# A separate tile for Gelu's quarters, and row spectra loaded for two pairs at a time, in a Fourier-operator kernel

## The reference, cut to what matters

```python
h = einsum('bhwi,ic->bhwc', x, fc0_w) + fc0_b            # 3 channels -> 64
for l in range(4):
    xf  = rfft2(h)
    top = einsum('bixy,ioxy->boxy', xf[:, :, :16, :16],  w1[l])   # mixes channels, mode by mode
    bot = einsum('bixy,ioxy->boxy', xf[:, :, -16:, :16], w2[l])
    sc  = irfft2(top and bot in a spectrum of zeros)
    y   = sc + einsum('bihw,oi->bohw', h, pw_w[l]) + pw_b[l]
    y   = (y - mean) * rsqrt(var + 1e-5) * gamma[l] + beta[l]     # mean, var of a channel over all images
    h   = gelu(y)
h   = gelu(h @ fc1_w + fc1_b)
out = h @ fc2_w + fc2_b
```

## Time and profile before

| | |
|---|---|
| median of 3 runs | 4079.1 us |
| the profiled execution | 4098.0 us |
| its span, first to last instruction | 4096.2 us |
| PE busy | 3206.6 us (78%) |
| DVE busy | 2414.7 us (59%) |
| ACT busy | 2249.3 us (55%) |
| fused stage of layer 0 | 262 to 905 us |
| fused stage of layer 1 | 1118 to 1740 us |
| fused stage of layer 2 | 1950 to 2572 us |
| last stage | 2797 to 3400 us |

### The profile page before, as it was taken

One profiled execution on the slowest core, in us unless ns is written; L12 is line 12 of the kernel. 1 busy time (PEld: TensorE's weight loads), 2 busy tenths in 40 slices (PEclk: granted clock), 3 DMA queues, 4 the chain that ended last, 5 costly groups with the idle time before them and its releaser, 6 DMA issues. The chain is left out here.

```text
span 4096.2 us, 119274 instructions
## 1 busy us (share of the span) xinstructions
PE 3206.6 (78%) x52804; PEld 1856.2 (45%) x52804; DVE 2414.7 (59%) x2482; ACT 2249.3 (55%) x2652; POOL 173.7 (4%) x249
## 2 busy tenths in 40 slices
PE   6678888886677777867777777678999994869786
PEld 4544444444544444446444444464444442733532
DVE  4555555555677778856778877564333333554556
ACT  3655565665566566656656666565666663222321
POOL 2013200000000000000000000000010012000000
PEclk9899999998899999988899999898999997779688
DMA  8877766668878889888889988886434320011062
GB/s 284 321 207 184 180 157 154 166 159 296 282 246 257 259 237 279 240 308 297 247 240 273 280 253 230 291 303 219 168 127 162 131 86 12 1 43 42 1 118 60
DMA packets 174127, 798.69 MB, mean 195 GB/s; under 512 B 32137, under 2 KB 38609, under 8 KB 124270
## 3 DMA queue, kind: packets, MB, share of 16 engines
q1 hardware_dynamic: 161628, 774.61, 61.9%
q0 software_dynamic: 7936, 13.65, 1.1%
q10 hardware_dynamic: 4050, 2.74, 0.2%
HBM read 445.01 MB, written 342.23 MB: 192 GB/s over the span
## 5 line engine op out<-in xcount | busy, mean ns | idle before, releaser
L906 PEld LDWEIGHTS bank<-fb,arena 64*64 64x64 f32 x16384 | 558.6, 196 | 548.1 <-issue 491.7
L906 PE MATMUL bank<-fb,arena 64*64 64x128 f32 x16384 | 622.6, 290 | 201.3 <-issue 146.5
L923 DVE TENSOR_TENSOR arena<-bank,arena 128x1024 f32<-128x1024 f32 x384 | 467.7, 1218 | 426.6 <-PE bank L906 425.9
L1142 ACT ACTIVATE arena<-bank 128x1024 f32<-128x1024 f32 x384 | 384.0, 1023 | 535.0 <-PE bank L1064 313.3
L1185 DVE STREAM_TRANSPOSE arena<-arena 128x1024 f32<-128x1024 f32 x384 | 458.4, 1212 | 136.7 <-ACT arena L1132 134.8
L915 DVE STREAM_TRANSPOSE arena<-bank 128x1024 f32<-128x1024 f32 x256 | 318.7, 1245 | 327.7 <-PE bank L896 327.4
L1064 PE MATMUL bank<-arena,wst 64*64 64x512 f32 x3072 | 420.1, 631 | 24.3 <-issue 16.6
L1149 ACT ACTIVATE arena<-arena 128x1024 f32<-128x1024 f32 x384 | 403.1, 1050 | 0.3
L1135 ACT ACTIVATE arena<-arena,shift,scale 128x1024 f32<-128x1024 f32 x256 | 316.5, 1236 | 116.1 <-DVE arena L923 114.4
L896 PE MATMUL bank<-arena,ga 64*64 64x256 f32 x4096 | 304.2, 405 | 94.4 <-DVE arena L923 28.4
L637 PE MATMUL bank<-arena 64*64 64x128 f32 x8192 | 276.0, 282 | 92.9 <-issue 63.8
(11 more groups left out here) (240 smaller groups left out, 3641.2 us busy)
## 6 DMA issues: line engine op xcount, KB each, us to landing
y_dram<-arena SPq DMA_DIRECT2D x384, 512.0 KB, 8.2
arena<-y_dram SPq DMA_DIRECT2D x96, 2048.0 KB
spec_out<-arena SPq DMA_DIRECT2D x128, 512.0 KB, 10.6
arena<-in_w_modes SPq DMA_DIRECT2D x28, 2048.0 KB, 14.9
arena<-spec_out SPq DMA_DIRECT2D x112, 512.0 KB, 10.9
arena<-spec_in SPq DMA_DIRECT2D x24, 2048.0 KB, 9.7
spec_in<-arena SPq DMA_DIRECT2D x96, 512.0 KB, 8.4
spec_in<-arena SPq DMA_DIRECT2D x8, 2048.0 KB, 13.4
```

What stands on the lines that cost most here:

```text
L906: mm = pe.matmul(hpx(bank[2 * s + i][CHAN[v], :])[:, :, j * S:(j + 1) * S], a2[p % 2][CHAN[i], :, v, 4 * T + j], hpx(fb2[CHAN[i], :]), sta ...
L923: dve.tensor_tensor(chunk(p, T), slot(s), chunk(p, T), ALU.add).then_inc(y_added, 1)
L1142: act.activation(chunk(p, T), slot(NEXT_SLOT[T]), ACT.Copy).then_inc(evicted, 1)
```

## The change

Two things change, and the code of TensorE's steps is put in another form.

*Gelu's result gets a tile of its own.* `hidden_of(T)` is a quarter of `h_at`, one tile for the current pair, which takes part of the space that the second spectra buffer had. Gelu writes `hidden_of(T)`; `px_turn` and `next_of` read it. `evict` still writes `chunk(p, T)`. It now waits for Gelu (`h_made`) in place of the transpose (`px_turned`). Gelu of a quarter waits until the transpose and the next-layer product of the same quarter of the pair before are done.

*Spectra come for two pairs.* `grp` is one buffer of 1 MB for two pairs, where it was two buffers of four pairs each. `spec_out` is laid out by pairs, so the load has runs of 1 KB. `next_rows` in step n, for odd n alone, waits for the row products of pair n and then loads pairs n+1 and n+2 whole. The mixing's transposes write `m_sb` in the new order.

At the end of a stage the first weights are loaded one step later, and one of the two others behind the last store, because their places overlap the new tiles. TensorE's steps are now calls of one function `step(m, u)` with m the number of two pairs; it can hold a loop's variable, but here it is called for every pair in turn, so that the program remains written out.

```diff
-        spec_out = nc.dram_tensor("spec_out", [NCH, P, NG, GI * C], F32, kind="Internal").ap()
+        spec_out = nc.dram_tensor("spec_out", [NCH, P, NP, 2 * C], F32, kind="Internal").ap()
...
-                    dve.transpose(m_sb[c % 2][:, 4 * j:4 * j + 4, v, :], modes[:, 32 * j:32 * j + 32]).then_inc(mixed_turned, 1)
+                    dve.transpose(m_sb[c % 2][:, 16 * j:16 * j + 16, v, :].rearrange("p (g q) (a o) -> p g a q o", q=Q, a=2),
+                                  modes[:, 32 * j:32 * j + 32]).then_inc(mixed_turned, 1)
...
-        grp = [at(u * PX, M2, GI, HB) for u in range(2)]
+        grp = at(0, NCH, 2, 2 * C)
+        h_at = at(PX, 2, PX // 2)
...
+        hidden_of = lambda T: h_at[:, :, T * BK:(T + 1) * BK]
...
-        def load_piece(sp, l, n):
-            if n // Q + 1 < NG:
-                load_group(sp, l, n // Q + 1, slice(n % Q * (NCH // Q), (n % Q + 1) * (NCH // Q)))
+        def load_rows(sp, m, cs):
+
+            sp.dma_start(grp[:, cs].rearrange("p c u x -> p c (u x)"),
+                         spec_out[cs, :, 2 * m:2 * m + 2].rearrange("c p u x -> p c (u x)")).then_inc(grp_loaded, 16)
+
+        def next_rows(sp, l, n):
+            if n % 2 == 1 and n + 1 < NP:
+                sp.wait_ge(rows_done, (l * NP + n + 1) * 2)
+                sp.sem_inc(waited[sp.engine], 1)
+                load_rows(sp, (n + 1) // 2, slice(0, NCH))
...
-            load_piece(sp, l, 0)
             for n in range(NP + 2):
-                if n + 1 < NP:
-                    load_piece(sp, l, n + 1)
+                next_rows(sp, l, n)
                 if n > 1 and (n - 2) % Q == Q - 1:
                     store_spectra((n - 2) // Q)
-                if n == NP - 2:
+                if n == NP - 1:
+                    sp.wait_ge(rows_done, (l * NP + NP) * 2)
+                    sp.sem_inc(waited[sp.engine], 1)
                     load_modes(sp, l + 1, 0)
...
                 if 0 < n <= NP:
                     store(n - 1)
+                if n == NP:
+                    sp.wait_ge(px_turned, (l * NP + NP) * 4)
+                    sp.sem_inc(waited[sp.engine], 1)
+                    load_weights(sp, l + 1, 1)
...
             def gelu(p, T):
+                if p > 0:
+                    act.wait_ge(px_turned, n * 4 + T - 3)
+                    act.wait_ge(next_done, n * 4 + T - 3)
...
-                    act.activation(chunk(p, T), chunk(p, T), ACT.Gelu, bias=shift[:], scale=scale[:]).then_inc(h_made, 1)
+                    act.activation(hidden_of(T), chunk(p, T), ACT.Gelu, bias=shift[:], scale=scale[:]).then_inc(h_made, 1)
...
             def evict(p, T):
-                act.wait_ge(px_turned, n * 4 + T + 1)
+                act.wait_ge(h_made, n * 4 + T + 1)
                 act.wait_ge(next_done, n * 4 + T + 1)
```

More of the change, by code:

```diff
@@ L483, in build @@
         r_sb = [at(R_AT + u * B * MC, NG, MC * GI) for u in range(2)]
-        m_sb = [at(M_AT + u * (2 * B * HB + 8 * BK), NG, 2, GI * HB) for u in range(2)]
+        m_sb = [at(M_AT + u * (2 * B * HB + 8 * BK), NP, 2, 2 * HB) for u in range(2)]
         x2 = [at(X_AT + 4 * BK * v, 4 * BK) for v in range(2)]
@@ L540, in store @@
                 sp.sem_inc(waited[sp.engine], 1)
[L541 to L545, removed]
+                if c >= NCH - 2:
+                    for t in range(4):
+                        row = t % 2 * C + t // 2 * HB
+                        sp.dma_start(grp[row:row + HB, c],
+                                     m_sb[c % 2][t * HB:(t + 1) * HB, 0:2].rearrange("p q v x -> p q (v x)")).then_inc(grp_loaded, 16)
                 if c == NCH - 2:
@@ L881, in load_x, with inner, rows @@
                              ).then_inc(p_loaded[p % NS], 16)
-        def load_piece(sp, l, n):
-            if n // Q + 1 < NG:
-                load_group(sp, l, n // Q + 1, slice(n % Q * (NCH // Q), (n % Q + 1) * (NCH // Q)))
[L887 to L890, removed]
+        def inner(m):
+            return not isinstance(m, int)
+        def rows(pe, l, m, u, hc, s):
+            if hc == 0 and u == 0:
+                pe.wait_ge(grp_loaded, l * (GRP_LOADS * 16) + (m * 16 + 9 * 16))
                 pe.sem_inc(waited[pe.engine], 1)
@@ L1032, in y_of @@
                 pe.sem_inc(waited[pe.engine], 1)
-                mm = spectral(pe, p, T, Y_SLOT[T], not first)
+                mm = spectral(pe, u, T, Y_SLOT[T], not first)
                 if first:
@@ L1090, in h_dft, with step @@
                             mm = pe.matmul(bank[4 + c][CHAN[v], 256:512], ghq[QUAD[c], k * 2 * K1:(k + 1) * 2 * K1],
-                                           t1[p % 2][QUAD[c], hh * 2 + v, :, :, ri * M2:(ri + 1) * M2],
+                                           t1[u][QUAD[c], hh * 2 + v, :, :, ri * M2:(ri + 1) * M2],
                                            start=(k == 0), stop=(k == 3), tile_position=(32 * c, C * v))
                 mm.then_inc(hdft_done, 1)
+            def step(m, u, now=True, before=True, after=True, older=True):
+                last = (m - 1, 1) if u == 0 else (m, 0)
+                then = (m, 1) if u == 0 else (m + 1, 0)
+                if before:
+                    next_of(*last, 2)
+                if now:
+                    y_of(m, u, 0)
+                    y_of(m, u, 1)
+                if after:
+                    rows_of(*then, 0)
+                if older:
+                    h_dft(m - 1, u)
+                if before:
+                    next_of(*last, 3)
+                if now:
+                    y_of(m, u, 2)
+                if after:
+                    rows_of(*then, 1)
+                if before:
+                    w_dft(*last)
+                if now:
+                    next_of(m, u, 0)
+                    next_of(m, u, 1)
+                    y_of(m, u, 3)
@@ L1095, in tensor_fuse @@
             pe.wait_ge(mixed_turned, (l * NU + NU - 1) * 2)
             pe.sem_inc(waited[pe.engine], 1)
-            rows_of(0, 0)
+            rows_of(0, 0, 0)
             tensor_sums(pe, l)
-            rows_of(0, 1)
-            for n in range(NP + 2):
-                now, before, after = n < NP, 0 < n <= NP, n + 1 < NP
-                if before:
-                    next_of(n - 1, 2)
-                if now:
-                    y_of(n, 0)
-                    y_of(n, 1)
-                if after:
-                    rows_of(n + 1, 0)
-                if n > 1:
-                    h_dft(n - 2)
-                if before:
-                    next_of(n - 1, 3)
-                if now:
-                    y_of(n, 2)
-                if after:
-                    rows_of(n + 1, 1)
-                if before:
-                    w_dft(n - 1)
-                if now:
-                    next_of(n, 0)
-                    next_of(n, 1)
-                    y_of(n, 3)
+            rows_of(0, 0, 1)
@@ L1124, in scalar_fuse @@
+            step(0, 0, before=False, older=False)
+            step(0, 1, older=False)
+            for m in range(1, NP // 2 - 1):
+                for u in range(2):
+                    step(m, u)
+            step(NP // 2 - 1, 0)
+            step(NP // 2 - 1, 1, after=False)
+            step(NP // 2, 0, now=False, after=False)
+            step(NP // 2, 1, now=False, before=False, after=False)
         def scalar_fuse(act, l, first):
@@ L1184, in px_turn @@
                     dve.wait_ge(wdft_done, n - 1)
-                dve.transpose(hT[p % 2].rearrange("p i h s c -> p i (h s c)")[:, :, T * BK:(T + 1) * BK], chunk(p, T)).then_inc(px_turned, 1)
+                dve.transpose(hT[p % 2].rearrange("p i h s c -> p i (h s c)")[:, :, T * BK:(T + 1) * BK], hidden_of(T)).then_inc(px_turned, 1)
             def w_turn(p, i):
@@ L1295, in rows_of @@
                     pe.wait_ge(rows_turned, R + 1)
-                rows(pe, l, p, hc, 0)
+                rows(pe, l, p // 2, p % 2, hc, 0)
             def y_of(p, T):
```

88 lines of the change are left out of this document (42 added, 46 removed).

## The result

The changed kernel takes 4374.5 us (median of 4 runs, 4372.2 to 4377.6) against 4078.0 us for the kernel before (median of 4 runs now, where 3 gave 4079.1): a ratio of 1.0725, 95% interval [1.0706, 1.0743]. The forecast was 4348. The profiled execution has a span of 4372.7 us, 276.5 us more than before.

A forecast was written before the change was run, and what follows sets the result against it. Layers 1 and 2 were taken as near a transfer limit, DMA 85 to 86% busy. 231 + 30 + 8 = +269 us on the profiled 4098.0 gave 4367, less 19 for the median: 4348 us; range 4200 to 4480.

The forecast's parts named there:

- The step that carried it: Layers 1 and 2: spectra load queued behind store and pair's load lands after TensorE wants it; 231 us with its corrections.
- Rivals 1 and 4: 1: load not held behind the others, about 4120 us, chance 0.08; 4: change does nothing, 4079 us, chance 0.04.
- rival 2: Delays add up: spectra store delays every second load fully, clock falls each time; 14.3 us a load, 4563 us, chance 0.07.
- Rival 3: Eviction waiting for the transpose was the brake, so the change gains; about 3946 us, chance 0.03.
- The 8.2: Layers 1 and 2: us per load that it lands after TensorE wants it, at 1187.4 against 1179.20.
- The 1.5 for the spectra's store: Layers 1 and 2: us per load added because four pairs' spectra are stored after every second load; ends 0 and 4.2.
- Given back: Layers 1 and 2: TensorE's instructions arrive while it waits, saving 3.0 us a load, at most 4.6.
- 1.0 for the clock: Layers 1 and 2: us per load for TensorE's granted clock falling after a pause; between 0 and 1.9.
- forecast 30: Layer 0: load lands at 508.6, a wait of 2.0 us for each of 15 loads, 30 us.
- Forecast +8: Layer ends: first weights load later ahead of needed spectra, while starting loads shrink; +8 us in all, ends -11 and +25.
- the bound of 2212: Mixing's transpose L770 writing runs of 32 elements: at worst 2212 ns instead of 1226; the forecast took 0 cost.
- The sum of +269 us: Whole kernel: 231 for layers 1 and 2, 30 for layer 0, 8 for layer ends, on the profiled 4098.0 us.

The follow-up runs named there:

- two buffers: Changed kernel plus a second row-spectra buffer of two pairs, each load issued two pairs earlier; 4095.8 us, ratio 1.0016 to the kernel before.
- two slots of one pair: Changed kernel with its 1 MB for row spectra used as two slots, one pair loaded each step; 4109.9 us, ratio 1.0050 to the kernel before.
- load first: Changed kernel, one buffer, its 1 MB spectra load issued ahead of the store and the pair's load; 4099.9 us, ratio 1.0030 to the kernel before.
- Gelu in place: Changed kernel, one buffer, Gelu writing back into the pair's tile and eviction waiting for the transpose; 4375.8 us, ratio 1.071 to the kernel before.
- both undone: Changed kernel with two spectra buffers of two pairs and Gelu in the pair's tile; 4093.5 us, ratio 1.0020 to the kernel before.
- run 20: Not a run's label: words of "a run 20 us above its median", the unchanged kernel's profiled execution, 4098.0 us against a median of 4079.1.

## Why the prediction was right

*Where.* The step that carried it, that the load stands third in a queue and is wanted after 10.4 us, is shown by three experiments that each take away one of its conditions: a longer lead (two buffers, or two slots of one pair) or a better place (load first). Each removes the loss but for 0.2 to 0.5%. Rivals 1 and 4 fall with the landings of 11.4 us and more, rival 2 with 7.6 us a load in place of its 14.3. Rival 3 falls with the runs with Gelu in place.

*How much, layers 1 and 2.* Per load, in layer 1: the profile has 147.7 / 15 = 9.8 us of waiting; the prediction had 8.2 + 1.5 = 9.7. That these agree is luck, for each of the two terms was off. The 8.2 was too small. The load shown above is waited for 11.0 us: the store now starts with the second row products (1642.70 and 1642.75) where it was 1.3 us ahead of them, the three transfers take 0.7 us longer than the 21.0 worked out, and the 0.76 us for which TensorE idled before the first row products anyway are now part of the wait. The 1.5 for the spectra's store was too large. That store stands in the two steps ahead of six of the 14 loads waited for in layer 1. By the timeline TensorE waits 10.5 us for these six in the mean (5.7, 13.5, 13.4, 3.4, 10.8 and 16.3) and 10.6 us for the other eight; in layer 2 it is 12.1 and 10.7. The six loads do land later, but they are also issued earlier, as seen from where TensorE is: it wants them 8.7 us after their issue in the mean, and the others after 3.4. Given back: all named waits of PE in layer 1 sum to 137.5 us before and 248.5 after; without the 147.7 there are 100.8, so 36.7 us came back, 2.4 a load (3.0 in the prediction). 26.7 of these are L1090, now L1100, by "issue" (38.5 to 11.8). That TensorE's instructions arrive while it waits, as the prediction had it, fits this; the trace does not name what ends such a wait. What is left of the stage's +114 us is 3 us, 0.2 a load, where the prediction had 1.0 for the clock. At a single wait the clock costs more, 2.6 us: after 1664.56 the 16 row products and 64 of L1100 take 1.98 + 3.71 us, where 1.09 and 1.98 are usual. That the net is small fits the other pauses, and their slow stretches, having gone; it is not tested. The sum came out at 7.6 us a load for 7.7. In layer 2, with the same views, it is 10.5 of waiting, 2.6 back and 0.1 left, 8.0 a load.

*Layer 0.* Waits 26.6 us, forecast 30; but the stage grew by 39. The step that was mis-sized is the clock: I priced it in layers 1 and 2 alone, 30 us, and it cost most where I had put nothing. TensorE's busy time for the same products grew by 4.3 us in layer 1, by nothing in layer 2, and by 19.4 in layer 0 (545.3 to 564.7 us). The listed waits of layer 0 grew from 105.4 to 123.5 us, 18.1, so 8.5 of the 26.6 us came back, which I had not counted there either. A wait of 1.84 us at 601.33 is followed, 17 us later, by a slow stretch that the same pair's products do not have in the kernel before. TensorE in layer 0 of the changed kernel:

```profile
601.33 1.09 PE L897 MATMUL bank<-arena,ga 64*64 64x256 f32 x16 [1.84 <-DMA arena<-spec_out]
...
617.87 1.20 PE L908 MATMUL bank<-fb,arena 64*64 64x128 f32 x32 [2.35 <-issue]
618.85 1.93 PE L1044 MATMUL bank<-arena,wx 64*64 64x512 f32 x8
620.45 2.03 PE L908 MATMUL bank<-fb,arena 64*64 64x128 f32 x32
```

And the same products of the same pair before, L1037 and L906:

```profile
604.16 1.20 PE L906 MATMUL bank<-fb,arena 64*64 64x128 f32 x32 [2.35 <-issue]
605.14 1.08 PE L1037 MATMUL bank<-arena,wx 64*64 64x512 f32 x8
606.00 1.13 PE L906 MATMUL bank<-fb,arena 64*64 64x128 f32 x32
```

The pause of 2.4 us stands in both, and no slow stretch followed it before. The granted clock of the slow one, from the changed kernel's stage table (the column before the last two):

```profile
618.80:622.20 3.40, 3.40 (x52) 2.38 (x49) 0.24 (x1) 1.21 (x2) 0.00 (x0) 0.52 0.02 5
```

That is about the lower of the two levels. Such a stretch costs some 1.7 us. Counting products that take over 0.25 us more than is usual for their line, layer 0 has 10 such stretches before and 19 after. They are not all behind loads, and some stand in the kernel before too, after the same pause of 2.4 us. But the runs say that the waits bring the additional ones: Gelu in place keeps the waits and has 19, load first, two buffers and both undone have 9 each, two slots 10. Layer 0 of the runs with the load first and with Gelu in place:

```profile
261.00:899.00 638.00, 545.36 (x10634) 303.60 (x10649) 343.47 (x309) 386.79 (x484) 71.38 (x73) 0.97 0.62 168
```

```profile
265.00:944.00 679.00, 563.14 (x10634) 308.72 (x10650) 343.63 (x309) 386.81 (x484) 71.31 (x73) 0.95 0.64 158
```

*Layer ends, transposes, short runs.* Forecast +8. From the last row product of a layer to the first of the next, the three stretches changed by +1.0, -5.8 and +4.8 us, nothing in sum; ahead of layer 0 the span lost 4.7 us, and behind the last row products it gained 5.5. L770 takes 1222 ns (median) with runs of 32 elements, for 1226 ns in the mean before: the bound of 2212 was never near. The run with both undone puts all of these together at 0.2% [-0.04, 0.44].

*The whole.* The sum of +269 us stands against 276.5 us of span. The forecast of 4348 is 26 us short of 4374.5 all the same: the kernel before was profiled in a run 20 us above its median, the changed one at its median, and the prediction took 19 us off.

*The page's estimate.* The Trainium skill's "DMA: Bandwidth & Descriptors", section "Anatomy of one DMA", fits one transfer on the GpSimd path; the estimate by it was 14.0 us for the 5 MB. The trace has 21.7 for three transfers on SyncE's queue, 241 GB/s, and the measurement decides.

## What to carry to other kernels

Before a buffer is taken from a load, add up what stands in front of that load in its queue at the moment when its buffer comes free, and lay the sum beside the time until it is wanted: here 21 us against 10, which no busy share shows. If memory is short, the cure is lead or place, not bytes: smaller slots that come free one at a time, or the wanted load issued ahead of stores that nobody waits for. When a kernel is near the DMA limit, try the run length of its largest store by itself.

## What the runs showed that I had not expected

Stores to DRAM with shorter runs were faster: a pair's 2 MB in runs of 8 KB is the kernel before, in runs of 4 KB at the same place in the queue 1.6% less time [0.9812, 0.987], in runs of 2 KB, each issued when its quarter is ready, 2.4% less [0.9728, 0.9784]. How much of the last step is length and how much is the earlier issue wasn't tried; in layer 1 the rate of the busy engines is the same at both, 319 GB/s, so it does not speak for the length. Nor was it tried whether the number of transfers that a store is made of plays a part: the halves have eight where there were four, the quarters sixteen. I had expected that short runs could only cost.

And in layer 0 new waits of 2 us at every second pair cost nearly as much again in clock, 19.4 us of busy time for 26.6 us of waits, in slow stretches that can begin at a later pause, 17 us behind the wait. The runs without the waits have TensorE busy for 543.9 us (two buffers) and 545.4 us (load first) there, the two with them for 564.7 and 563.1.
